# Early routed blocks in two stages and through two quarters, weight splits moved ahead and mostly to VectorE, in a routed decoder layer

## What is computed

```
x = layernorm(x + attention(x))          # 16 heads that share one score matrix of rank 64
x = layernorm(x + mlp_e1(x))             # expert e1 of 4 by the token's id; hidden width 256
x = layernorm(x + p * mlp_e2(x))         # expert e2 = top-1 of a softmax router over 4
mlp(x) = (silu(x Wg) * (x Wu)) Wd        # third step: width 1024
```

## Time and profile before

| | us |
|---|---|
| median of 3 runs (lowest, highest) | 196.0 (195.14, 196.38) |
| the profiled execution, its own time | 197.44 |
| its span | 195.3 |
| PE busy, share of the span | 176.0, 90% |
| DVE, ACT, POOL busy | 126.8, 103.9, 112.0 |
| mean granted clock of PE | 0.986 |

### The profile page before, as it was taken

How to read it: one execution, slowest core, us unless ns; L and a number is a source line. 1 busy time by engine, 2 the same in 40 slices (tenths; PEclk the granted TensorE clock), 3 DMA queues, 4 the chain that set the end, 5 groups by cost and what they waited for, 6 DMA issues and landing times.

```text
span 195.3 us, 3893 instructions
## 1 busy us (share of the span) xinstructions
PE 176.0 (90%) x969; PEld 139.7 (72%) x969; DVE 126.8 (65%) x398; ACT 103.9 (53%) x274; POOL 112.0 (57%) x138
## 2 busy tenths in 40 slices
PE   1999997999999698989999999999999999999810
PEld 0877775357878463768888878888888888888610
DVE  3179987814678686745664374444799986888950
ACT  3136877535467837346773955653566522355530
POOL 7015366779826765446873068880588810277783
PEclk9999999999999999999999999999999999999995
DMA  5999999246998223044544305454040000011010
GB/s 154 361 342 419 378 363 313 90 142 174 313 365 352 86 88 89 22 124 130 193 157 134 138 0 163 162 163 166 0 143 21 0 0 3 0 54 57 23 62 24
DMA packets 15317, 29.14 MB, mean 149 GB/s; under 512 B 1726, under 2 KB 11968, under 8 KB 15170
## 3 DMA queue, kind: packets, MB, share of 16 engines
q1 hardware_dynamic: 13568, 25.68, 39.3%
q0 software_dynamic: 1440, 3.22, 4.7%
q10 hardware_dynamic: 290, 0.01, 0.1%
HBM read 20.41 MB, written 9.28 MB: 152 GB/s over the span
## 4 chain that ended last, share of the span: by engine, by line
PE 74%; POOL 10%; issue 7%; DMA 3%; DVE 2%; ACT 1%; another core or an unknown queue 1%; POOLq 1%; SPq 0%; DVEq 0%; ACTq 0%
PE bank L477 14%; PE bank L478 13%; PE bank L479 13%; POOL out_tokens L466 5%; PE bank L722 4%; PE bank L587 4%; PE bank L622 4%; PE bank L556 4%; PE bank L645 3%; PE bank L491 2%; POOL rstd L389 2%; PE bank L565 2%; PE bank L485 2%; PE bank L535 2%; DMA x_sorted<-buf,slot 2%
## 5 line engine op out<-in xcount | busy, mean ns | idle before, releaser
L385 POOL TENSOR_TENSOR w_lo<-stage,w_hi 128x512 fp32r<-128x512 f32 x48 | 61.3, 1301 | 43.8 <-ACT w_hi L796 43.8
L905 ACT ACTIVATE gate<-bank 128x256 f32<-128x256 f32 x44 | 17.0, 386 | 47.9 <-PE bank L479 44.6
L1194 DVE TENSOR_TENSOR hid<-bank,gate 128x256 f32<-128x256 f32 x44 | 18.7, 425 | 29.9 <-ACT gate L905 29.6
L477 PE MATMUL bank<-w_hi,xr 128*128 x88 | 35.9, 408 | 1.3 <-DVE xr L1157 0.8
L478 PE MATMUL bank<-w_lo,xr 128*128 x88 | 34.5, 392 | 0.0
L479 PE MATMUL bank<-w_hi,xr 128*128 x88 | 34.5, 392 | 0.0
L477 PE MATMUL bank<-w_hi,hT 128*128 x88 | 28.3, 322 | 0.7 <-DVE hT L1199 0.7
L796 ACT ACTIVATE w_hi<-stage 128x512 fp32r<-128x512 f32 x48 | 28.6, 630 | 0.3 <-PE bank L479 0.3
L478 PE MATMUL bank<-w_lo,hT 128*128 x88 | 24.7, 281 | 0.0
L479 PE MATMUL bank<-w_hi,hT 128*128 x88 | 24.7, 281 | 0.0
L477 PEld LDWEIGHTS bank<-w_hi,xr 128*128 128x128 f32 x88 | 16.6, 188 | 4.7 <-issue 2.5
(11 more groups left out here) (181 smaller groups left out, 324.2 us busy)
## 6 DMA issues: line engine op xcount, KB each, us to landing
stage<-in_w_ffn SPq DMA_DIRECT2D x16, 768.0 KB, 4.5
rows<-x_sorted SPq DMA_DIRECT2D x22, 132.0 KB, 2.3
x_sorted<-padrow SPq DMA_DIRECT2D x1, 2244.0 KB
x_sorted<-padrow SPq DMA_DIRECT2D x1, 2112.0 KB
buf<-in_x_tok SPq DMA_DIRECT2D x1, 1024.0 KB, 10.8
w_hi<-in_ctx SPq DMA_DIRECT2D x1, 1024.0 KB, 11.5
w_hi<-in_ctxT SPq DMA_DIRECT2D x1, 1024.0 KB, 14.1
x_sorted<-padrow SPq DMA_DIRECT2D x1, 792.0 KB, 12.6
```

The lines of the kernel that those rows point to most:

```text
L385: g.tensor_tensor(out=lo, in0=src, in1=hi.bitcast(F32), op=ALU.subtract).then_inc(split_lo, 1)
L477: mm(dst, xhi, whi, start=start, stop=False)
L905: a(gate[:, (T + j) % 2, :], fA[j % 2][:, 0:FQ], ACT.Silu).then_inc(silu_done, 1)
L1194: v.tensor_tensor(out=hid[:, (T + j) % 2, :], in0=fA[j % 2][:, FQ:2 * FQ], in1=gate[:, (T + j) % 2, :], op=ALU.mult).then_inc(h_done, 1)
```

## The change

It does these things.

- Routing of phase 2 has three stages: blocks 0 and 1 after tiles 0 to 4, block 2 after tiles 5 and 6, the other eight after tile 10. Each has its own counts on PE, tables on DVE (`tables_a`, `tables_b`, `tables_late`) and wait on SP.
- The order of items begins (0,0), (0,1), (1,0), (1,1), (0,2), (1,2) as (block's quarter, block); then the rest of quarters 0 and 1, then 2 and 3. The two quarters of the early blocks add up in one PSUM bank (OPENS, CLOSES), so three evictions less.
- The phase 2 matrices move from w_hi to the arena over phase 1's x; their load waits on SP for the last `z_of` of phase 1.
- The chunks of quarters 0 and 1 are loaded straight into w_lo, without `stage`, and split there. All 24 of their pieces are split before or in phase 2 and its end.
- Low parts: POOL 0-3, 8, 19 of the first 24, DVE the other 18, with eight of them (4, 5, 6, 7, 9, 10, 11, 12) in one run right before `hidden(0)`. In quarter 2 DVE takes 4 of 12, in quarter 3 none. Quarter 2's 12 pieces are split two per item over items 14 to 19.
- The fill of scr2 is one transfer of 33 blocks, issued after the 11 sorted rows and the load of chunk 7.
- The first part of each engine's order is written out by hand, and the `idle_products` between phase 2 and phase 3 are gone (12, 6 and 3 matmuls).

```
@@ constants
-ROUTED = 7
+STAGE_ENDS = (5, 7, T)
+STAGE_BLOCKS = ((0, 2), (2, 3), (3, T))
+EARLY_ITEMS = [(0, 0), (0, 1), (1, 0), (1, 1), (0, 2), (1, 2)]
+ITEMS = EARLY_ITEMS + [(q, t) for q in (0, 1) for t in range(3, T)] + [(q, t) for q in (2, 3) for t in range(T)]
+LO_BY_DVE = (4, 5, 6, 7, 9, 10, 11, 12, 13, 14, 15, 16, 17, 18, 20, 21, 22, 23, 26, 29, 32, 35)
+        SHARE = {q: s for q, s in ((2, [2, 2, 2, 2, 2, 2]), (3, [0, 1, 1, 2, 1, 2, 1, 2, 1, 1, 0]))}
@@ sync
+            def load_direct(n):
+                sp.dma_start(w_lo[:, o:o + CHUNK].bitcast(F32), wffn_in[n]).then_inc(d_direct[n], 16)
...
-            load_chunk(2)
+            for n in range(2, E + 2):
+                load_direct(n)
+            sp.wait_ge(z_done, BATCH)
             sp.dma_start(ctx4[:, :, :, E:E + D], ...).then_inc(d_ctx, 16)
-            load_chunk(3)
-            sp.dma_start(pads2[:, 0:HALF2, :], ...).then_inc(d_init2, 16)
+            load_direct(E + 2)
...
-            sp.dma_start(pads2[:, HALF2:BLOCKS2, :], ...).then_inc(d_init2, 16)
-            for n in range(E, E + SLOTS):
+            load_direct(E + 3)
+            sp.dma_start(scr2.rearrange("(p r) c -> p r c", p=P),
+                         padrow[:].unsqueeze(1).broadcast_to([P, BLOCKS2, ROW])).then_inc(d_init2, 16)
+            for n in range(2 * E, 2 * E + SLOTS):
                 load_chunk(n)
@@ gpsimd
+            split(8)
             validity()
+            split(19)
             root2(0)
             root2(1)
-            pool.wait_ge(d_init2, 32)
+            pool.wait_ge(d_init2, 16)
+            scatter2(0)
+            scatter2(1)
+            scatter2(2)
+            scatter2(3)
             root2(2)
+            scatter2(4)
             root2(3)
+            scatter2(5)
+            scatter2(6)
             root2(4)
+            scatter2(7)
...
@@ tensor (end of phase 2)
+            th(10)
+            add(9)
+            rank(2)
+            down(9)
+            add(10)
             ftx(0)
+            down(10)
+            ftx(1)
+            fup(0)
+            fup(1)
+            rank(3)
+            fth(0)
+            fup(2)
+            rank(4)
+            ftx(2)
+            fth(1)
+            fdown(0)
+            fup(3)
+            fth(2)
+            fdown(1)
+            fup(4)
+            fth(3)
+            fdown(2)
+            fup(5)
+            ftx(3)
+            fth(4)
+            ftx(4)
+            fdown(3)
+            fup(6)
...
@@ scalar (end of phase 2)
+            silu(10)
+            shift2(2)
+            h1copy(9)
+            h1copy(10)
+            evict(9)
+            norm2(5)
+            norm2(6)
             fxhi(0)
+            shift2(3)
+            evict(10)
+            fxhi(1)
+            fsilu(0)
+            norm2(7)
+            fsilu(1)
...
@@ vector
+            split(4)
...
+            split(12)
+            hidden(0)
+            hidden(1)
+            split(13)
+            split(14)
+            split(15)
+            hidden(2)
+            residual(0)
...
+            residual(6)
+            tables_a()
+            hidden(9)
+            residual(7)
+            hidden(10)
+            choose(2)
+            residual(8)
+            place(2)
+            tables_b()
+            fxlo(0)
+            choose(3)
+            fxlo(1)
+            residual(9)
+            residual(10)
+            fhidden(0)
+            split(21)
+            place(3)
+            fhidden(1)
+            choose(4)
+            fhlo(0)
+            split(22)
+            place(4)
...
```

More of the change, by code:

```diff
@@ L265, in route_kernel @@
         CONSTS = 23
-        items = [(q, t) for q in range(NQ) for t in range(T)]
+        items = ITEMS
         block = ctx.enter_context(nc.Block())
@@ new lines, in _ @@
+            fup(1)
+            rank(3)
+            fth(0)
+            fup(2)
+            rank(4)
+            ftx(2)
[13 more added lines that the diff above has]
+            fup(6)
+            fth(5)
+            fdown(4)
+            ftx(5)
+            fup(7)
+            ftx(6)
@@ new lines, in _ @@
+            fth(6)
+            fdown(5)
+            ftx(7)
+            fup(8)
+            fth(7)
+            fdown(6)
+            fup(9)
+            ftx(8)
+            fth(8)
+            fdown(7)
+            fup(10)
+            fth(9)
+            ftx(9)
+            fdown(8)
+            fup(11)
+            ftx(10)
+            fth(10)
+            fdown(9)
+            fup(12)
+            fth(11)
+            fdown(10)
+            fup(13)
+            fth(12)
+            fdown(11)
@@ L762, in _ @@
+            for i in range(WRITTEN_OUT, len(items) + 2):
+                if i < len(items):
+                    fup(i)
+                if i <= len(items):
+                    fth(i - 1)
+                fdown(i - 2)
         @block.scalar
@@ new lines, in _ @@
+            split(18)
+            split(19)
+            h1copy(3)
+            x1copy(6)
+            silu(5)
+            h1copy(4)
+            x1copy(7)
+            shift2(0)
+            silu(6)
+            norm2(0)
+            h1copy(5)
+            x1copy(8)
+            split(20)
+            silu(7)
+            norm2(1)
+            split(21)
+            h1copy(6)
+            norm2(2)
+            x1copy(9)
+            silu(8)
+            shift2(1)
+            split(22)
+            norm2(3)
@@ new lines, in _ @@
+            residual(3)
+            choose(0)
+            residual(4)
+            hidden(6)
+            place(0)
+            split(20)
+            hidden(7)
+            choose(1)
+            residual(5)
+            hidden(8)
+            place(1)
+            residual(6)
[9 more added lines that the diff above has]
+            choose(3)
@@ new lines, in _ @@
+            fhidden(5)
+            fxlo(4)
+            fhlo(4)
+            fxlo(5)
+            fhidden(6)
+            fhlo(5)
+            fsum(3)
+            fhidden(7)
+            fhlo(6)
+            fxlo(6)
+            fhidden(8)
+            fhlo(7)
+            fsum(5)
+            fxlo(7)
+            fhidden(9)
+            fxlo(8)
+            fsum(6)
+            fhlo(8)
+            fxlo(9)
+            fhidden(10)
+            fsum(7)
+            fhlo(9)
+            fhidden(11)
@@ L1253, in _ @@
+            fhlo(10)
+            fsum(8)
+            fxlo(10)
+            fhidden(12)
+            fsum(9)
+            fhlo(11)
+            fhidden(13)
+            fsum(10)
+            fsum(11)
+            fhlo(12)
+            for i in range(WRITTEN_OUT, len(items) + 3):
+                if i < len(items):
+                    fhidden(i)
+                if i <= len(items):
+                    fhlo(i - 1)
+                if i <= len(items) + 1 - T:
                     fsum(i - 2)
-                if i == T + 1:
+                if i == WRITTEN_OUT + 3:
```

564 lines of the change are left out of this document (318 added, 246 removed).

## The result

| | before | after |
|---|---|---|
| median (lowest, highest), 4 runs each | 196.19 (195.14, 196.55) | 208.64 (208.25, 209.82) |
| span of the profiled execution | 195.3 | 208.1 |
| mean granted clock of PE | 0.986 | 0.958 |

The ratio is 1.063 (95% interval 1.059 to 1.067): 12.4 us slower. The forecast was 199.0 with a range up to 201.8; the direction was right, the size was four times too small.

What follows compares the result with a forecast made beforehand. It took PE's work to bound the kernel from 86.89 on, so only its start could move. Late blocks +1.1, refill +0.8 and clock +1.2 made +3.1: 196.0 to 199.1, said as 199.0, range 192.6 to 201.8.

Steps and rivals of the forecast that it cites:

- Part 1: Before phase 2's first scatter: the 33-block fill lands at about 64.8, POOL's wait ends at 65.0, against 60.51 before.
- The bound of 67: Upper bound on the fill wait's end: 2 us more than 65.0, for landing behind the write queue.
- Rival A: Faster: the fill is in before needed, scatters begin at 60.5, -2.6 in all, 193.4; chance 0.22.
- Part 2: From fill to PE: scatter of tile 4 issued at 71.4, PE's ftx(0) at 77.0, 0.7 later than before.
- Part 3: Late blocks: late rows issued at 90.3, ftx(3) at 92.6, work then ending at 184.7 against 183.6, so +1.1.
- Rival C: No change: late rows' path 2 us shorter and the clock stays full, +0.3, 196.3; chance 0.16.
- Part 4: Low parts on DVE before phase 3: 0.65 us a piece, hidden(0) 0.3 late, no loss.
- Rival B: Slower: VectorE bounds phase 2 if a subtraction takes 1.0 or more; with the fill 201.5; chance 0.14.
- Its sign: What would show VectorE as the bound of phase 2: hidden(10) later than 69.
- Part 5: Refill of quarter 2's weights: ACT's split waits for item 13's fdown and holds fsilu(15); +0.8, bounds 0 and 2.5.
- Rival D: Quarter 2's refill stalls on chunk 11 and again on chunks 12 to 14: 199.9; chance 0.08.
- Part 6: PE's clock without idle products: probably falls in the empty stretch before ftx(0); +1.2, bounds 0 and 4.1.

Runs made afterwards that it cites:

- e13: The changed kernel with its fill cut from 33 blocks to the five this case's inputs read as pads: 202.95 us, ratio 1.029 to the kernel before.
- e12: The changed kernel itself run again, nothing edited: 209.1 us (two runs, 208.64 and 209.55).
- e16: The changed kernel with the five-block fill of e13 and chunk 7 loaded ahead of the sorted rows: 200.64 us, ratio 1.019 to the kernel before.
- e2: The changed kernel with chunk 7 loaded ahead of the sorted rows, full fill kept: 207.19 us, ratio 1.049 to the kernel before.
- e7: The changed kernel with the run of eight low parts back on POOL, behind phase 1's last scatter: 208.56 us, ratio 1.052 to the kernel before.
- e5: The changed kernel with quarter 2's splits an item later, items 15 to 20: 208.35 us, ratio 1.052 to the kernel before.
- e6: e5 with ACT's exp for the gates also moved right behind fxhi(10): 207.24 us, ratio 1.046 to the kernel before.
- e17: e16 plus the refill of e9 (five-block fill, chunk 7 early, quarter 2 re-split, exp moved): 197.86 us, ratio 1.006 to the kernel before.
- e9: The changed kernel with quarter 2's split shares 0, 3, 2, 2, 2, 1, 2 and exp behind fxhi(10): 206.23 us, ratio 1.047 to the kernel before.
- e8: The changed kernel with 8 idle matmuls before th(3) and 14 before th(10): 209.09 us, ratio 1.054 to the kernel before.

## Why the prediction was right in direction and wrong in size

By the item clock the 12.8 us are: the fill some 6 (6.3 between after and e13 at item 14, of which 1.0 is e13's earlier phase 1; 6.0 between e12 and e13, of which 0.3), chunk 7 some 2 (2.1 between e13 and e16, though e16's phase 1 ends 0.5 later), the refill 5.6 (item 14 to 18), a rest of 0.4 behind item 18; and the two stages' own gain, -1.5 (e16 at item 14). The parts were taken off one behind the other, so what two of them share stands with the first. In the forecast's own sum two terms were too small: up to item 14 it had 1.1 + 1.2 = 2.3, and 6.8 was measured; for the refill it had 0.8, and 5.6 was measured.

**Part 1, the fill: right mechanism, mis-sized.** 65.0 was said for the first scatter, 70.33 measured. Step by step: the pads were to begin at 50.0 + 2.0 = 52.0, and their first packet is at 53.36, 1.4 later. Chunk 7 was priced at 404 GB/s, and it moved at 215 where it was alone. The pads were to take 12.8 at the measured rate, and from the first packet to the last (68.92) they took 15.6, 2.8 more: a rate over windows in which a transfer has all engines leaves out its two ends, where it shares them. The old fill had shown it too: its windows end at 56.6, but there its last packet ended at 58.05. Landing behind the last packet took 0.55, where 0.2 was in the sum, 0.3 more. And from landing to POOL's scatter passed 70.33 - 69.47 = 0.9, which was not in it at all. 1.4 + 2.8 + 0.3 + 0.9 = 5.4, the 5.3 that were missing. That SP was 0.8 late in after (48.79 against 47.99) is none of it: in e12 it is not late, and the fill lands at the same time:

```profile
47.99 0.43 SPq L321
48.46 20.91 DMA x_sorted<-padrow
```

The bound of 67 had 2 us for landing, of which 0.55 came, and nothing for the three others. Rival A, a fill in time, fell with it.

**Part 1 again, a sentence that was wrong:** "The direct loads do not disturb phase 1" is true to the letter, but they disturb phase 2. Before, the chunks came through `stage` and were never awaited there. Now chunk 7 is loaded behind the rows and its split stands in ACT's order: some 2 us (e16). No part of the forecast asked when chunk 7 lands.

**Part 2, from scatter to PE, held.** 77.0 - 65.0 = 12.0 was said; PE's ftx(0) came 11.3 behind the first scatter (81.63). The hole of PE that it foresaw is there, from 73 to 77.5, ended by `h1copy` behind shift2(2):

```profile
77.52 0.66 PE L673 MATMUL bank<-ident,hid 128*128 128x128 f32 x2 [4.58 <-ACT arena L979]
```

**Part 3, the late blocks, held as a chain:** ftx(3) was to be 15.6 behind ftx(0), and came at 97.58, 15.9 behind. The gain of the two stages was overrated: rival A gave 3.4 with the fill in time (its -2.6 less the 0.8 of the refill); e16 shows 1.5 at item 14. In e16 item 0 is 2.2 early, item 11 still 1.2: and ftx(3) is at 89.23 where it was at 85.49. Of the 5.0 us of work that is done before it (97.1 against 92.1 left), the longer path to the late rows takes 3.7 back. (Rival C's +0.3 does not come out of its own terms, which give 3.1 - 1.2 - 2 = -0.1; the forecast does not rest on it.)

**Part 4, VectorE, held.** 0.65 a piece was said; the group in after (ns min/median/max) and the run:

```profile
L293 DVE TENSOR_TENSOR w_lo<-w_lo,w_hi x18: 658/684/2201, 40.3 to 93.9; 128x512 fp32r<-128x512 f32 x18
```

```profile
40.28 6.42 DVE L293 TENSOR_TENSOR w_lo<-w_lo,w_hi 128x512 fp32r<-128x512 f32 x8
46.62 0.74 DVE L1274 TENSOR_TENSOR hid<-bank,gate 128x256 f32<-128x256 f32 x2
```

The run was 6.4, not 5.2 (its sixth piece, at 43.29, took 2.20 us beside POOL's split at 43.62), and began 0.4 later, so hidden(0) is 1.9 late (46.62 against 44.75) and not 0.3. Rival B is out by its own condition, a subtraction of 1.0 or more. Its sign, though, came: hidden(10) was to be B if later than 69, and it is at 72.82.

```profile
72.82 0.43 DVE L1274 TENSOR_TENSOR hid<-bank,gate 128x256 f32<-128x256 f32 x1 [0.26 <-issue]
```

The sign did not tell VectorE from other delays of phase 2. In e12, with the full clock over 58 to 62, hidden(10) is at 70.93, and in e2, with chunk 7 early as well, at 68.55: of the 5.1 us against before, about 1.9 come with the lower clock and about 2.4 with chunk 7, and 0.8 are left for VectorE and all else. That none of it reached the end is shown for after, where the fill came last (e7); without the fill it was not tested.

**Part 5, the refill, is the second failure.** 0.8 was said with bounds 0 and 2.5; it is 5.6. The wait for fdown of item 13 was the right one, but it cost 2.2, not 0.8. The exp and its two table loads were a term left out: the change moved the exp from item 11 (`i == T`) to `i == WRITTEN_OUT + 1`, item 15, among the pairs of splits. Before, it stood at 108.3 to 111.1 in ACT's timeline with one split behind. It costs 2.3 at item 16 in after (2.7 in e5, nothing in e6). The rest, 1.1, comes at items 17 and 18, where two more pairs of splits stand; its cause was not tested apart. The mended refill of e17 gives back 3.3 of the loss (e16 against e17 at the last item). Chunk 11 was said to be in "about when wanted"; it costs nothing in after (+12.4 to +12.6) only because all else is late, and 1.6 to 3.7 where that is mended (e9, e6). Rival D had the right place with 2 us, but another cause: chunks 11 to 14, not fdown and exp.

**Part 6, the clock.** It fell, as forecast, and once more at 58 to 62. The first fall cost nothing at the end: e12 is without it, its hidden(10) is 1.9 earlier, but the first scatter waits for the fill (70.22 against 70.33) and item 14 is within 0.2. For the second fall 1.2 was in the sum, and no pair of runs shows it. In after and in e12, which is at the lower level longer (0.50 over 74 to 80 against 0.56), item 0 comes 16.1 and 16.2 behind the first scatter; in e13, where the granted clock is full throughout, it comes 80.36 - 63.23 = 17.1 behind. But these differ in more than the clock, and e8 didn't hold it, so the price stays open, with no sign of a large one.

## What to carry to other kernels

When a transfer moves behind others in one queue, add up every byte ahead of it at the rate of its own pattern and place (here 200 to 230 GB/s for the rows, 215 for the chunk behind them, 341 for the pads), add the two ends at which it shares the engines with its neighbours (2.8 us here), the landing and the consumer's start, and then ask the same of each transfer that it passes. When an order of work is rewritten, list what is tied to an index in it (here the exp with two table loads) and cost each instruction at its new place. And compare two traces by an event that occurs once per item: here the delays show at once that nearly half of the loss is not at the fill. Take a second trace of the same kernel first: here it had the end of phase 1 0.8 us earlier and one fall of the clock fewer.

## What the runs showed of the hardware that was not expected

- One subtraction of VectorE with both inputs in SBUF took 7.80 us beside a row of POOL's splits of 1.2 us each, not the length of one of them. The Trainium skill (SBUF — State Buffer, "Who interferes with whom") says that it waits for the instruction of GpSimd that holds the port; here its one record lasts to 54.83, past the end of the whole row at 54.27, so it waited for the instructions behind that one as well.
- 4.46 MB of pads ran at 341 GB/s while alone, but from their first packet to their last took 15.6 us (53.36 to 68.92), 287 GB/s: weight packets of the transfers before and behind moved at the same time at both ends. The landing came 0.55 us behind the last packet (0.56 in e12).
- Chunk 7 landed 7.4 us behind its issue in e13, though its 0.79 MB are 2.0 us at 404 GB/s; it stood behind the sorted rows.
- The granted clock was at its lower level after PE was empty for 2.35 us (57.6 in after), and again behind a hole of 4.58 (77.5). It stayed full behind holes of 2.85 us at the same place in e12 and of 2.74 in e13, so the length of the hole alone did not decide.
